# Turning P in one go, and projecting gates and values of the feed-forward in one run, in a hand-scheduled attention and feed-forward kernel

## The reference, cut to what matters

```python
for i in range(DEPTH):                                   # DEPTH = 6
    x = attn_layer(shift_tokens(x), Wqkv[i], q_scale[i], k_scale[i], Wo[i]) + x
    x = ffn_layer(shift_tokens(x), ln_g[i], ln_b[i], W1[i], b1[i], W2[i], b2[i]) + x

# attn_layer: 16 heads of 64, windows of 32 queries that see their own and the previous window
q = l2norm(q) * qs;  k = l2norm(k) * ksc;  q, k = rotated by position
sim = where(mask, -max, einsum('bhwie,bhwje->bhwij', q, k) * 8)
out = softmax(sim) @ v;  return out @ Wo
# ffn_layer: a and gate have 341 features each
a, gate = split((layernorm(x) * g + bln) @ W1 + b1);  return a * gelu(gate) @ W2 + b2
```

## Time and profile before

| | us |
|---|---|
| median of 3 runs | 1722.73 |
| lowest, highest | 1717.05, 1724.04 |
| the profiled execution | 1714.45 |
| its span | 1712.6 |

### The profile page before, as it was taken

The page is one execution under the profiler, slowest core; times in us unless marked ns, Lnnn a source line. Parts: engine busy times, 40 slices in busy tenths (PEclk is TensorE's granted clock), DMA queues, the critical chain, the costliest instruction groups (busy, mean ns, idle before and its releaser), DMA issues.

```text
span 1712.6 us, 89331 instructions
## 1 busy us (share of the span) xinstructions
PE 1613.6 (94%) x36892; PEld 1250.3 (73%) x36892; DVE 1333.5 (78%) x1952; ACT 1282.2 (75%) x2104; POOL 1066.3 (62%) x783
## 2 busy tenths in 40 slices
PE   7896688999999999999999999999999999999996
PEld 3574567777777777777777777777777777777775
DVE  5576667787888878888888888887887888888863
ACT  4794456788787778877778777788777788787873
POOL 2202656568676768666668667678676677776641
PEclk9898899999999999999999999999999999999998
DMA  2000423222422322423322422223322222332220
GB/s 99 2 0 1 131 52 74 54 68 68 129 69 54 72 69 58 125 64 73 72 49 70 129 69 62 61 71 76 107 68 71 68 65 74 72 73 66 65 57 26
DMA packets 75728, 116.79 MB, mean 68 GB/s; under 512 B 17294, under 2 KB 27276, under 8 KB 74764
## 3 DMA queue, kind: packets, MB, share of 16 engines
q1 hardware_dynamic: 75660, 115.99, 27.3%
HBM read 19.04 MB, written 1.05 MB: 12 GB/s over the span
## 4 chain that ended last, share of the span: by engine, by line
PE 89%; issue 5%; ACT 3%; DVE 2%; DMA 0%; POOL 0%; ACTq 0%; DVEq 0%; SPq 0%
PE ps L600 15%; PE ps L821 10%; PE ps L714 10%; PE ps L799 9%; PE ps L764 9%; PE ps L718 8%; PE ps L717 8%; PE ps L882 4%; PE ps L757 3%; PE ps L843 2%; PE ps L845 2%; PE ps L844 2%; PE ps L833 2%; PE ps L828 2%; PE ps L589 1%
## 5 line engine op out<-in xcount | busy, mean ns | idle before, releaser
L412 POOL TENSOR_TENSOR arena<-arena,rnorm 128x1024 f32<-128x1024 f32 x192 | 361.8, 1906 | 347.6 <-ACT rnorm L1071 347.6
L403 POOL TENSOR_TENSOR arena<-arena 128x1024 f32<-128x1024 f32 x192 | 457.0, 2380 | 16.1 <-DVE arena L1422 12.4
L600 PEld LDWEIGHTS ps<-cst,arena 64*128 64x128 f32 x6656 | 243.3, 140 | 148.9 <-issue 140.1
L600 PE MATMUL ps<-cst,arena 64*128 64x64 f32 x6656 | 300.3, 230 | 25.2 <-ACT arena L1101 9.4
L1418 DVE TENSOR_TENSOR arena<-ps,rope 128x1024 f32<-128x1024 f32 x192 | 234.5, 1221 | 90.7 <-issue 79.8
L1107 ACT ACTIVATE arena<-ps 128x512 f32<-128x512 f32 x192 | 114.7, 597 | 174.3 <-PE ps L600 174.0
L1422 DVE TENSOR_TENSOR arena<-ps,rope 128x1024 f32<-128x1024 f32 x192 | 232.9, 1213 | 0.0
L718 PE MATMUL ps<-wqkv_hi,x_hi 128*128 128x512 f32 x576 | 230.0, 399 | 0.0
L717 PE MATMUL ps<-wqkv_lo,x_hi 128*128 128x512 f32 x576 | 229.4, 398 | 0.0
L1432 DVE TENSOR_REDUCE norm<-arena 128x16 f32<-128x1024 f32 x192 | 224.2, 1208 | 0.0
L714 PE MATMUL ps<-wqkv_hi,x_lo 128*128 128x512 f32 x576 | 214.8, 454 | 9.2 <-issue 7.5
(11 more groups left out here) (122 smaller groups left out, 2745.4 us busy)
## 6 DMA issues: line engine op xcount, KB each, us to landing
v_sb<-v_nat SPq DMA_DIRECT2D x576, 130.0 KB, 2.4
v_sb<-v_nat SPq DMA_DIRECT2D x192, 65.0 KB, 2.0
wqkv_sb<-wqkv SPq DMA_DIRECT2D x6, 1536.0 KB, 6.4
v_sb<-v_sb SPq DMA_DIRECT2D x96, 65.0 KB, 2.0
wo_sb<-wo SPq DMA_DIRECT2D x6, 512.0 KB, 8.1
w_sb<-w SPq DMA_DIRECT2D x6, 341.0 KB, 7.8
x<-xT SPq DMA_DIRECT2D x1, 1024.0 KB, 5.0
scl<-scales SPq DMA_DIRECT2D x6, 128.0 KB, 7.6
```

Source lines behind the costliest of these rows:

```text
L403: pool.tensor_tensor(t_cos[:, m, j, :], t_cos[:, m, j, :], t_sin[:, j, :], ALU.add)\
L412: pool.tensor_tensor(x, x, rnorm[:, H * j:H * j + H].unsqueeze(2).to_broadcast([P, H, D]), ALU.mult).then_inc(s[done], 1)
L600: mm = pe.transpose(ps[0:width, bank + t, 64 * c:64 * c + 64], src[r], ident[r, r], tile_position=(64 * t, 0))
```

## The change

- TensorE: P is turned in one go of 16 transposes in each half, ahead of the output projection (first half) and of `down` (second half). Gates and values are projected in one run of 18 matmuls, behind q: gate 2 and value 2 to bank 7, gates 0 and 1 to bank 6, values 0 and 1 to bank 1. The output projection is one run of 16. k comes behind it, directly ahead of attend, and waits for the feed-forward's products, because it writes banks 6 and 7.
- ScalarE: both exponentials come first, then the table load and the gates, then one copy of P (128x1024 instead of two of 128x512), then the other table load. In the second half both exponentials, the copy and `high` come ahead of `round_norm` and of the roundings of weights.
- VectorE: in the first half `products` and `residual` come between the rope products of q and those of k.

```diff
@@ tensor
-            def k(pair, m, gates=False):
+            def k(pair, m, over_gates=False):
-                if gates:
-                    pe.wait_ge(s["f_gated"], CREDIT + 3 * (pair - 1 - LAG) + 1)
+                if over_gates:
+                    pe.wait_ge(s["f_prod"], CREDIT + 3 * (pair - 1 - LAG) + 3)
-            def turn_p(pair, m, g):
+            def turn_p(pair, m):
-                if g == 0:
-                    pe.wait_ge(s["centred"], CREDIT + 2 * n + 2)
-                else:
-                    pe.wait_ge(s["p_copied"], CREDIT + 2 * n + 1)
-                pe.wait_ge(s["exped"], CREDIT + 2 * n + g + 1)
+                pe.wait_ge(s["centred"], CREDIT + 2 * n + 2)
+                pe.wait_ge(s["exped"], CREDIT + 2 * n + 2)
-                for hh in range(4):
-                    mm = turn(4, hh, s_sb[:, g, 2 * hh:2 * hh + 2, :].rearrange("p c k -> p (c k)"))
+                for h in range(H // 2):
+                    mm = turn(4, h, s_sb[:, h // 4, 2 * (h % 4):2 * (h % 4) + 2, :].rearrange("p c k -> p (c k)"))
...
-            def gates_up(f):
+            def all_up(f):
                 pe.wait_ge(s["f_split"], CREDIT + f + 1)
                 pe.wait_ge(s["w1_ready"], CREDIT + f + 1)
                 pe.wait_ge(s["v_copied"], CREDIT + 2 * (f + LAG) + 2)
-                up(ps[:, 7, 0:N], 1, 2).then_inc(s["f_gate_up"], 1)
+                up(ps[:, 7, 0:N], 1, 2)
+                up(ps[:, 7, N:2 * N], 0, 2).then_inc(s["f_gate_up"], 1)
+                up(ps[:, 6, 0:N], 1, 0)
+                up(ps[:, 6, N:2 * N], 1, 1).then_inc(s["f_gate_up"], 1)
                 pe.wait_ge(s["centred"], CREDIT + 4 * (f + LAG) + 1)
-                up(ps[:, 1, 0:N], 1, 0)
-                up(ps[:, 1, N:2 * N], 1, 1).then_inc(s["f_gate_up"], 1)
-            def values_up(f):
-                pe.wait_ge(s["f_gated"], CREDIT + 3 * f + 3)
                 up(ps[:, 1, 0:N], 0, 0)
-                up(ps[:, 1, N:2 * N], 0, 1).then_inc(s["f_value_up"], 1)
-                pe.wait_ge(s["att_done"], CREDIT + f + LAG)
-                up(ps[:, 0, 0:N], 0, 2).then_inc(s["f_value_up"], 1)
+                up(ps[:, 1, N:2 * N], 0, 1).then_inc(s["f_value_up"], 2)
@@ tensor slot, first half
                 if ff:
-                    gates_up(g - LAG)
+                    all_up(g - LAG)
+                turn_p(g, 0)
                 if out:
-                    project_out(g - 1, 0)
-                if ahead:
-                    k(g + 1, 0, gates=ff)
-                turn_p(g, 0, 0)
-                if out:
-                    project_out(g - 1, 1)
-                turn_p(g, 0, 1)
-                if ff:
-                    values_up(g - LAG)
+                    project_out(g - 1)
+                if ahead:
+                    k(g + 1, 0, over_gates=ff)
                 attend(g, 0, 0)
@@ second half
-                turn_p(g, 1, 0)
+                turn_p(g, 1)
                 if ff:
                     down(g - LAG)
-                turn_p(g, 1, 1)
@@ scalar
-            def copy_p(pair, m, g):
+            def copy_p(pair, m):
-                act.activation(p_t[:, 4 * g:4 * g + 4, :].rearrange("p c (t k) -> p t c k", t=2),
-                               pair_of_banks(2)[:, :, 0:4 * SPAN].rearrange("p t (c k) -> p t c k", c=4),
-                               ACT.Copy)\
+                act.activation(p_t.rearrange("p c (t k) -> p t c k", t=2),
+                               pair_of_banks(2).rearrange("p t (c k) -> p t c k", c=8), ACT.Copy)\
@@ scalar slot
+                exps(g, 0, 0)
+                exps(g, 0, 1)
                 if ff:
                     act.preload_act_table_set("gelu_and_others")
                     gates(g - LAG)
+                copy_p(g, 0)
+                if ff:
                     act.preload_act_table_set("natural_log_exp_and_others")
-                exps(g, 0, 0)
                 if after == 7:
                     round_weights(layer, 2)
-                copy_p(g, 0, 0)
-                exps(g, 0, 1)
                 if ahead:
                     high(g + 1, 1)
-                copy_p(g, 0, 1)
...
                 exps(g, 1, 0)
+                exps(g, 1, 1)
+                copy_p(g, 1)
+                if more:
+                    high(g + 2, 0)
                 if norm:
                     round_norm(g - 2)
                 if after == 6:
                     round_weights(layer, 0)
+                    round_weights(layer, 1)
                 if after == 2:
                     round_up(layer)
-                copy_p(g, 1, 0)
-                exps(g, 1, 1)
-                if more:
-                    high(g + 2, 0)
-                copy_p(g, 1, 1)
-                if after == 6:
-                    round_weights(layer, 1)
@@ vector slot, first half
                 centre(g, 0, 1)
                 if ahead:
                     rope_products(g + 1, 0, 0)
-                    rope_products(g + 1, 0, 1)
+                if ff:
+                    products(g - LAG)
                 if out:
                     residual(g - 1)
-                if ff:
-                    products(g - LAG)
+                if ahead:
+                    rope_products(g + 1, 0, 1)
                 normalise(g, 0, 0)
```

More of the change, by code:

```diff
@@ L787, in attend @@
                     pe.wait_ge(s["v_moved"], CREDIT + 16 * (18 * pair + 8 + 10 * m))
-                    pe.wait_ge(s["p_copied"], CREDIT + 2 * n + 2)
+                    pe.wait_ge(s["p_copied"], CREDIT + n + 1)
                     pe.sem_inc(s["pe_waited"], 1)
@@ L811, in turn_o, with project_out @@
                 mm.then_inc(s["o_turned"], 1)
[L813 to L820, removed]
+            def project_out(pair):
+                pe.wait_ge(s["o_copied"], CREDIT + 2 * pair + 2)
+                pe.wait_ge(s["w_a_loaded"], 16 * layer_of(pair) + 16)
+                pe.wait_ge(s["centred"], CREDIT + 4 * pair + 5 if not isinstance(pair, int) or pair < SLOTS - 1
+                           else CREDIT + 4 * pair + 4)
+                for c in range(H // 2):
                     mm = pe.matmul(ps[:, 0, 0:N], wo_sb[:, c, :], o_t[:, c, :], start=(c == 0),
                                    stop=(c == H // 2 - 1), skip_group_check=True)
-                if half:
-                    mm.then_inc(s["projected"], 1)
+                mm.then_inc(s["projected"], 1)
             def mean(f, bank=1):
@@ L958, in _ @@
             pe.wait_ge(s["f_done"], CREDIT + SLOTS - LAG)
-            project_out(SLOTS - 1, 0)
-            project_out(SLOTS - 1, 1)
+            project_out(SLOTS - 1)
             down(SLOTS - 3, 7)
@@ L1101, in exps @@
                 act.activation(v, v, ACT.Exp).then_inc(s["exped"], 1)
-            def copy_p(pair, m, g):
+            def copy_p(pair, m):
                 n = 2 * pair + m
-                act.wait_ge(s["p_turned"], CREDIT + 2 * n + g + 1)
+                act.wait_ge(s["p_turned"], CREDIT + n + 1)
                 act.wait_ge(s["attended"], CREDIT + 2 * n)
-                act.activation(p_t[:, 4 * g:4 * g + 4, :].rearrange("p c (t k) -> p t c k", t=2),
-                               pair_of_banks(2)[:, :, 0:4 * SPAN].rearrange("p t (c k) -> p t c k", c=4),
-                               ACT.Copy)\
+                act.activation(p_t.rearrange("p c (t k) -> p t c k", t=2),
+                               pair_of_banks(2).rearrange("p t (c k) -> p t c k", c=8), ACT.Copy)\
                    .then_inc(s["p_copied"], 1)
@@ L1142, in round_norm, with gates @@
                 act.activation(f_hi[:, :], f_y, ACT.Copy).then_inc(s["f_high"], 1)
-            def gates(f, gate_2=7, gates_01=1):
+            def gates(f, gate_2=7, gates_01=6):
                 act.wait_ge(s["p_h_loaded"], 16 * layer_of(f) + 16)
@@ L1445, in centre @@
                 dve.wait_ge(s["maxed"], CREDIT + 2 * n + g + 1)
-                dve.wait_ge(s["p_turned"], CREDIT + 2 * n)
+                dve.wait_ge(s["p_turned"], CREDIT + n)
                 dve.tensor_tensor(s_sb[:, g, :, :].rearrange("p (h a) k -> p a h k", a=2), src,
@@ L1473, in subtract_mean, with products @@
                 dve.tensor_tensor(f_c, f_x, ps[:, bank, 0:N], ALU.subtract).then_inc(s["f_centred"], 1)
-            def products(f, values_01=ps[:, 1, :], value_2=ps[:, 0, 0:N]):
+            def products(f, values_01=ps[:, 1, :], value_2=ps[:, 7, N:2 * N]):
                 dve.wait_ge(s["f_down"], CREDIT + f)
```

## The result

The changed kernel takes 1754.83 us (median of four runs, 1753.11 to 1758.16), the kernel before on the same chip 1719.89 us (1711.89 to 1724.04). The medians lie 34.9 us apart; the ratio is 1.022, with a 95% interval of 1.0193 to 1.0247, which makes about 38 us slower. The profiled execution took 1758.16 us (span 1756.3), 43.7 more than the one of before. The forecast of 1770 us, slower, was right in direction and mechanism; it had 47 us added for the 38 of the ratio.

The account below looks back on a forecast made before the run. TensorE, 94% busy with no hole in the first half, was taken as the bound, with a new wait behind k: 40 x 1.04 = 41.6, other slots 5.6, together +47.2 us on the median 1722.73: 1770 us, range 1744 to 1785.

Parts of the forecast that it names:

- Steps 1 to 4: First half, TensorE, from the run of 18 matmuls through turn of P, output projection and k to attend: saves 0.43 us per slot.
- Steps 5 and 6: First half: k's late rope delays the first normalise's multiplication on VectorE, so the turn of q waits a new 1.44 us.
- Step 7: Rest of the first half keeps its durations, so the second half starts 1.04 us later.
- Covered work: Feed-forward products, copy of P, table load, small copies and squares of q end before TensorE asks for them: no added wait.
- The second half: TensorE saves about 0.6 us, costed at nothing because VectorE sets the end; bounds 0 to -0.25.
- (b): Five slots rounding the weights of q and k, both roundings now ahead of the squares: 0.6 us more each, +3.0.
- (c): Six slots rounding w1, now between the copy of P and the squares: 0.4 us more each, +2.4.
- (a): Four slots behind ScalarE's 2.47 us pause at the loop's end: -0.2 us each, -0.8 in all.
- (d): Slots 0 to 2, without feed-forward and with other stalls: +1.5 us (0 to +6).
- TensorE bounds all: Rival: k's lateness is hidden and both halves keep TensorE's savings, -1.0 us per slot, 1678 us; chance 0.05.
- Only v's wait: Rival: turn of q not held, only v waits for the squares of k; 0.3 us per slot, 1741 us; chance 0.11.
- The clock falls: Rival: TensorE's granted clock drops after the new waits, 3 us a slot, above 1850 us; chance 0.04.

Follow-up runs that it names:

- k_between: The changed kernel with k's projection back between the output projection's halves and, on VectorE, k's rope products ahead of the residual; ratio to before 0.9922.
- norm_later: The changed kernel with one more unused VectorE multiplication, 512 columns, between k's rope products and the first normalise; ratio to before 1.0642.
- norm_first: The changed kernel with the first normalise ahead of k's rope products on VectorE, k left late on TensorE; ratio to before 1.0786.
- second_only: The kernel before with only the change's second half: one turn and one copy of P, weight roundings behind that copy; ratio to before 1.0108.
- first_only: The kernel before with only the change's first half; second half keeps two turns and copies of P, roundings in old places; ratio to before 1.0347.
- second_early: second_only with the first rounding of weights, and that of w1, between the exponentials and the copy of P; ratio to before 1.0051.
- norm_bit_later: The changed kernel with one more unused VectorE multiplication, 128 columns, ahead of the first normalise; ratio to before 1.0329.
- k_between_pe: The changed kernel with k's projection between the output projection's halves on TensorE, residual still ahead of k's rope on VectorE; ratio to before 1.0637.

## Why the prediction was right, and where its sizes were off

**Steps 1 to 4, TensorE: right.** It forecast attend at slot start + 11.49; it came at + 11.54 (846.85 less 835.31), 0.38 earlier than before for the 0.43 forecast. Two small errors nearly cancel in it: k's matmuls took 1.36 to the last one (845.17 to 846.53) for 1.16, and the output projection 3.37 for 3.46. k_between, in which a common slot has no such wait, has 16.60 for the 16.94 of before: 0.34 saved, with one more step between kinds of matmul than the change has.

**Steps 5 and 6, the new wait: right.** The multiplication was forecast to end at + 15.01 and ended at + 15.00; the turn of q at + 15.14, and it started there. To the hundredth that is luck: the reciprocal came 0.06 later than forecast, and its multiplication 0.24 behind it instead of 0.31. The wait is 1.24 us by the modelled end of the turn of k, and 1.38 from that turn's start plus the 0.57 of the forecast, against 1.44. That this wait and no other sets the half is shown three ways: with k and its rope early on both engines, the half is 1.43 shorter (k_between); lengthened by 0.60, the slot is longer by 0.58 (norm_later); passed by on VectorE, the slot waits for v instead (norm_first).

**Step 7: right.** The second half starts at + 18.03, forecast + 17.98.

**Covered work: right.** The second table load ends at 844.66 and the squares of q at 846.37, and attend's 128 matmuls run on without a wait for them. The switch of tables takes 1.28 us here, and the next activation starts right behind it (843.38 + 1.28 = 844.66, then 844.68). The Trainium skill (ScalarE: Activation LUTs, What ACT_TABLE_LOAD costs) has about 1.28 for the load, which the trace bears out, and 1.38 more for a drain, 2.66 in all, of which no row here shows the drain.

**The second half: inside its bounds, not at the value taken.** I took 0, it gave 0.1: the step from the first reciprocal of a half to its multiplication on VectorE is 0.23, where before it was 0.32 (842.61 to 842.93 in the second half); the second pair has 0.23 in both. Merging the second half alone gave nothing (13.75 in second_only); beside the first half's merge it gave 0.2 a slot (31.87 to 31.67). That step says where: it is 0.32 or 0.33 in both halves of before, second_only, first_only and second_early, and 0.23 or 0.24 in both halves of all kernels with P in one part everywhere, so 0.09 in each half. What shortens it is open.

**The other slots.** (b) The rounding slots: forecast 1.04 + 0.6 = 1.64 more, measured 33.39 - 31.74 = 1.65. (c) w1's alone: the one such stretch that doesn't also hold a loop's end went from 30.66 to 32.17, 1.51 for a forecast 1.44. (a) with (c), across the loop's end: forecast - 0.2 + 0.4, measured 32.68 - 32.24 = + 0.44. The pause itself was 2.58 to 2.76 instead of 2.42 to 2.61, and the first half behind it is 0.40 to 0.58 longer than a common one, where I had 0.29. (d) Up to the residual that ends the fourth slot: forecast 2.9, measured 333.44 - 330.86 = 2.6. The last two slots: forecast + 0.5, measured - 1.7. The one before the last is 0.7 longer, the last 2.4 shorter. The last has no k and so not this wait; the 0.4 that TensorE saves in a slot is only a part of 2.4, and the rest is open.

**The sum.** Forecast + 47.2, measured + 43.7 between the two profiled executions: 32 common slots at 0.99 instead of 1.04 give - 1.5, the loop's ends + 1.0, the last two slots - 2.2, what follows the last residual - 0.5, the beginning - 0.3; the rest came as summed up. The medians lie 35 us apart, as the profiled execution of before was one of the shorter ones, and I had put the sum on the longer median.

**The rivals.** TensorE bounds all: false for the change, since k's last matmul starts at slot start + 11.22, a microsecond and a half behind the point from which that rival decides (826.2, which is + 9.7); but k_between, with k and its rope early again, is this case for the first half, which keeps 0.34; the second keeps 0.1 there and not the 0.6 of the rival, so a slot gains 0.42 and not 1.0. Only v's wait: false as well, the reciprocal started at + 14.1, and the rival needed it before 829.4, which is + 12.9. The clock falls: it didn't, in any of the 42 slots of the loop. But the argument for that (it holds through a wait of 1.10) was thinner than its chance of 0.04 said: with a wait 0.20 longer than the change's the clock fell in five slots (norm_bit_later), and with 0.61 more in 30, at 1.5 us a slot for the rival's 3 (norm_later). That the clock held is in part luck.

## What to carry to other kernels

Moving a projection on TensorE moves everything that the other engines do behind it in their written order: follow each queue to the instruction that a later matmul waits for, and move both sides or neither. A TensorE that is 94% busy pays out what it is spared only where nothing else has become late (the rest of the change is worth - 0.42 us a slot with k and its rope early, and + 0.98 with both late). Keep what others wait for at the front of a queue and put work with no reader near (roundings) where its engine idles.

## What the runs showed of the hardware

**A longer wait can cost twice.** In a stream that is otherwise dense, a wait of 1.24 us in each slot left the granted clock at 1.00 in all 42 slots of the loop (after), and 1.33 left it there in all but the four at the loop's end (first_only). With 1.44 it fell in five, four of them with a second wait of 2.3 (norm_bit_later); with 1.71 in 28 (k_between_pe), 1.85 in 30 (norm_later), 2.40 in 31 (norm_first). Where a stretch was looked at, it fell to the 1.2 GHz level for some 3 us of the work behind the wait; common slots with the lower clock are 1.2 to 1.5 us longer. The rounding slots show that a wait's length is not all: 2.26 us there left the clock alone in all five of the change, brought it down in two of five of k_between, and 2.31 in all five of second_only. What tells the slots of one kernel apart is open. The rule of the Trainium skill (Perfetto Trace Analysis, Matmul Optimizations), that matmuls should run back to back because the engine scales power by utilization, fits these rows.

**ScalarE's pause at the loop's end** was 2.42 to 2.90 us with one packet on the queue labelled "instruction" in it, and 4.68 to 5.39 us with two, in kernels whose text there hardly differs.
